# Second attention of a macaron block: value products issued inside the bursts, norm steps on GpSimd, no clearings, a squared term on VectorE

## What is computed

```python
q_norm_sq = jnp.sum(q * q, axis=-1, keepdims=True)
k_norm_sq = jnp.sum(k * k, axis=-1)[:, :, None, :]
qk = jnp.einsum('bhnd,bhmd->bhnm', q, k)
diff_sq = jnp.maximum(q_norm_sq + k_norm_sq - 2.0 * qk, 0.0)
denom = jnp.maximum((1.0 - q_norm_sq) * (1.0 - k_norm_sq), 1e-06)
cosh_arg = jnp.maximum(1.0 + 2.0 * diff_sq / denom, 1.0)
distance = arccosh(cosh_arg)
attn = jax.nn.softmax(-distance, axis=-1)
out = jnp.einsum('bhnm,bhmd->bhnd', attn, v)
```

## Time and profile before

| what | value |
|---|---|
| median of 3 runs | 3533.08 us (3528.67 to 3537.28) |
| the profiled execution's own time | 3532.39 us |
| its span | 3530.7 us |
| busy over the span: TensorE, VectorE, ScalarE, GpSimd | 2876.4, 2279.0, 1908.5, 850.3 us |
| mean granted clock of TensorE, as a share of full speed | 0.837 |
| the second attention (A1) in the span | about 1800 to 3090 us |
| its largest group, the GpSimd addition L1373, x96 in the page | 433.5 us, 4541 ns each |

### The profile page before, as it was taken

The page is one execution under the profiler, slowest core; times in us unless marked ns, Lnnn a source line. Parts: engine busy times, 40 slices in busy tenths (PEclk is TensorE's granted clock), DMA queues, the critical chain, the costliest instruction groups (busy, mean ns, idle before and its releaser), DMA issues. The chain is left out here.

```text
span 3530.7 us, 52885 instructions
## 1 busy us (share of the span) xinstructions
PE 2876.4 (81%) x17862; PEld 2183.2 (62%) x17862; DVE 2279.0 (65%) x5078; ACT 1908.5 (54%) x2244; POOL 850.3 (24%) x546
## 2 busy tenths in 40 slices
PE   5999968888599996999966767767676776679999
PEld 4888856666488885999952333333333333269998
DVE  5555557777555556666656776776676777366665
ACT  2222257676422222334318888887888888633333
POOL 1000010000000001000025555554655555410000
PEclk9999979999799997999975666666666666689999
DMA  2000000000000001000000000000000000010000
GB/s 78 0 0 0 0 1 1 0 0 0 0 1 0 0 0 48 0 0 0 0 0 0 1 1 0 0 0 0 0 0 0 0 0 0 0 48 0 0 0 24
DMA packets 3189, 17.98 MB, mean 5 GB/s; under 512 B 1088, under 2 KB 2112, under 8 KB 2112
## 3 DMA queue, kind: packets, MB, share of 16 engines
q1 hardware_dynamic: 3136, 17.32, 1.3%
HBM read 15.22 MB, written 2.10 MB: 5 GB/s over the span
## 5 line engine op out<-in xcount | busy, mean ns | idle before, releaser
L1373 POOL TENSOR_TENSOR A_Y<-A_Y,A_U 128x2048 f32<-128x2048 f32 x96 | 433.5, 4541 | 419.5 <-ACT A_U L1419 419.5
L1604 PE MATMUL ps<-A_QT,A_KT 9*128 9x512 f32 x512 | 294.3, 671 | 247.4 <-DVE A_U L1463 247.4
L1455 DVE TENSOR_SCALAR A_U<-ps 128x1024 f32<-128x1024 f32 x256 | 309.0, 1217 | 81.2 <-POOL A_Y L1373 50.4
L140 POOL TENSOR_TENSOR rstd<-var_eps,half_neg 128x4 f32<-128x4 f32 x45 | 49.8, 1107 | 1277.9 <-DVE var_eps L120 1277.9
L1604 PEld LDWEIGHTS ps<-A_QT,A_KT 9*128 9x128 f32 x512 | 120.0, 290 | 376.8 <-DVE A_U L1463 354.7
L1463 DVE SCALAR_TENSOR_TENSOR A_U<-ps,A_U 128x1024 f32<-128x1024 f32 x256 | 311.7, 1218 | 49.3 <-PE ps L1604 49.3
L1592 PE MATMUL ps<-A_QT,A_KT 28*128 28x512 f32 x512 | 269.7, 662 | 88.2 <-DVE A_U L1455 86.8
L257 ACT ACTIVATE F1b_act<-ps 128x512 f32<-128x512 f32 x256 | 153.3, 599 | 247.4 <-PE ps L223 231.4
L257 ACT ACTIVATE F1a_act<-ps 128x512 f32<-128x512 f32 x256 | 153.3, 599 | 242.9 <-PE ps L223 226.6
L257 ACT ACTIVATE F0b_act<-ps 128x512 f32<-128x512 f32 x160 | 95.7, 598 | 273.1 <-PE ps L223 273.1
L1419 ACT ACTIVATE A_U<-A_U 128x2048 f32<-128x2048 f32 x128 | 242.5, 1894 | 0.0
(11 more groups left out here) (334 smaller groups left out, 6673.0 us busy)
## 6 DMA issues: line engine op xcount, KB each, us to landing
dn<-in_down SPq DMA_DIRECT2D x2, 2048.0 KB, 12.0
stage<-in_up SPq DMA_DIRECT2D x1, 2560.0 KB, 9.2
X<-in_x SPq DMA_DIRECT2D x1, 2048.0 KB, 7.8
F1a_up<-in_up SPq DMA_DIRECT2D x1, 2048.0 KB, 7.8
F1b_up<-in_up SPq DMA_DIRECT2D x1, 2048.0 KB, 7.3
out_x<-X SPq DMA_DIRECT2D x1, 2048.0 KB, 6.3
dn<-in_down SPq DMA_DIRECT2D x1, 1280.0 KB, 11.9
qkv_w_s<-in_w_qkv SPq DMA_DIRECT2D x2, 192.0 KB
```

Source lines behind the costliest of these rows:

```text
L1373: eng.tensor_tensor(flat(y_slot(h)), flat(y_slot(h)), flat(Um[:, h % UR]), ALU.add).then_inc(s["t_ready"], 1)
L1455: eng.tensor_scalar(u_half(h, half), d_pair(n), 0.0, None, ALU.max).then_inc(s["dp_vector"], 1)
L1604: last = eng.matmul(ps[:, 4 + b, :], KT[r:r + 9, h // 2, kt * P:(kt + 1) * P], QT[r:r + 9, h // 2, :], start=True, stop=True)
```

## The change

In the second attention alone:

1. The value products of pairs 0, 2, 4 and 6 move from the stretch between the bursts into the burst before it (pair 0 into burst 1, 2 into burst 2, 4 into burst 3, 6 into the next pass's burst 0): a run of 8 behind half 5, another behind half 6. Pairs 1, 3, 5 and 7 stay between the bursts.
2. The residual sum goes to the buffer xa; GpSimd applies the norm (4 operations of 128 x 128) and copies the sum back to X. VectorE no longer applies the norm.
3. The clearings of the two tables go; TensorE, not VectorE, waits for `pad_ready`, before the first transposes.
4. Heads 4, 8 and 12 use the squared form.

```diff
-            SQUARED = ()
+            SQUARED = (4, 8, 12)
...
                 def square_on_vector(h):
-                    return h % 4 in SQUARED
+                    return h in SQUARED
...
+                def add_back_vector(eng, n, chunk):
+                    eng.wait_ge(s["o_done"], n)
+                    eng.tensor_tensor(xa[:, :].rearrange("p (t d) -> p t d", d=D), tiles_of(chunk),
+                                      ps[:, ROWS, :].rearrange("p (t d) -> p t d", d=D), ALU.add).then_inc(s["x_added"], 1)
+                    eng.drain()
+                    for t in range(TPC):
+                        eng.bn_stats(bn[:, t, :], xa[:, t * D:(t + 1) * D])
...
+                    eng.tensor_scalar(var_eps[:, :], mv[:, :, 1], EPS, None, ALU.add).then_inc(s["var_ready"], 1)
+
+                def apply_norm_gpsimd(eng, n, chunk):
+                    norm_gpsimd(eng, s, n)
+                    eng.drain()
+                    for t in range(TPC):
+                        eng.tensor_scalar(xn[:, t, :], xa[:, t * D:(t + 1) * D], mv[:, t, 0:1], rstd[:, t:t + 1],
+                                          ALU.subtract, ALU.mult)
+                    eng.drain().then_inc(s["xn_ready"], 1)
+                    eng.tensor_copy(tiles_of(chunk), xa[:, :].rearrange("p (t d) -> p t d", d=D))
+                    eng.drain()
...
                         eng.tensor_copy(xa[:, :], XT[:, 0:S]).then_inc(s["xa_ready"], 1)
-                        eng.memset(QA.rearrange("p h r -> p (h r)").bitcast(F32), 0.0)
-                        eng.memset(KA.rearrange("p h r -> p (h r)").bitcast(F32), 0.0)
-                        eng.memset(VA[:, :], 0.0)
-                        eng.drain()
                         eng.memset(QA[:, :, 26:28].bitcast(F32), 1.0)
...
+                        eng.memset(VA[:, :], 0.0)
+                        eng.drain()
...
                             if not first:
-                                norm_gpsimd(eng, s, c)
+                                apply_norm_gpsimd(eng, c, last_chunk(c))
...
                             if tail:
-                                residual_vector(eng, c, before_c)
-                                norm_stats_vector(eng, s, c, before_c)
+                                add_back_vector(eng, c, before_c)
                             out_copy_vector(eng, c, 0)
                             def after2(i):
-                                if tail and i == 1:
-                                    norm_apply_vector(eng, s, c, before_c)
...
-                        eng.wait_ge(pad_ready, 1)
                         take_q_vector(eng, 0, 6)
...
                             turn(c, EARLY)
-                            if not first:
-                                outputs(c - 1, 4, (0, 1))
                             turn(c, EARLY + 1)
-                            if not first:
-                                outputs(c - 1, 4, (2, 3))
...
                             def after0(i):
                                 if i < 4:
                                     turn(c, EARLY + 4 + i)
+                                if not first and i in (5, 6):
+                                    outputs(c - 1, 6, (2 * i - 10, 2 * i - 9))
...
                             if not first:
-                                outputs(c - 1, 6, (0, 1))
+                                outputs(c - 1, 7, (0, 1))
...
                             if not first:
-                                outputs(c - 1, 6, (2, 3))
-                                outputs(c - 1, 7, (0, 1, 2, 3))
+                                outputs(c - 1, 7, (2, 3))
...
                             def after1(i):
+                                if i in (5, 6):
+                                    outputs(c, 0, (2 * i - 10, 2 * i - 9))
...
-                            outputs(c, 0, (0, 1, 2, 3))
                             outputs(c, 1, (0, 1, 2, 3))
                             def after2(i):
+                                if i in (5, 6):
+                                    outputs(c, 2, (2 * i - 10, 2 * i - 9))
...
                             turn(c + 1, 0)
-                            outputs(c, 2, (0, 1))
                             turn(c + 1, 1)
-                            outputs(c, 2, (2, 3))
                             turn(c + 1, 2)
...
                             def after3(i):
                                 if i < 4:
                                     turn(c + 1, 4 + i)
+                                if i in (5, 6):
+                                    outputs(c, 4, (2 * i - 10, 2 * i - 9))
...
                         project_rows_tensor(eng, xa, 1, 7, "k_done")
+                        eng.wait_ge(pad_ready, 1)
```

More of the change, by code:

```diff
@@ L1169, in square_on_vector @@
                 def square_on_vector(h):
-                    return h % 4 in SQUARED
+                    return h in SQUARED
                 def squares(c, h):
-                    return c * (H // 4) * len(SQUARED) + len([i for i in range(h) if square_on_vector(i)])
+                    return c * len(SQUARED) + len([i for i in range(h) if square_on_vector(i)])
                 def flat(a):
@@ L1318, in early_bank @@
                     return (i + 2) % 6
-                (turn_out_tensor, divide_vector, turn_back_tensor, _, project_out_tensor,
-                 residual_vector) = tail_steps(s, lay, lambda t, g: OT[:, g, t * P:(t + 1) * P], on, oT, rden[:, :], ROWS)
+                (turn_out_tensor, divide_vector, turn_back_tensor, _, project_out_tensor, _) = tail_steps(s, lay, lambda t, g: OT[:, g, t * P:(t + 1) * P], on, oT, rden[:, :], ROWS)
                 def copy_back_vector(eng, n):
@@ L1332, in turn_norm_tensor @@
                     last.then_inc(s["tr_done"], 1)
+                def add_back_vector(eng, n, chunk):
[7 more added lines that the diff above has]
+                    for t in range(TPC):
+                        eng.bn_aggr(mv[:, t, :], bn[:, t, :])
+                    eng.drain()
[3 more added lines that the diff above has]
+                    eng.drain()
+                    for t in range(TPC):
+                        eng.tensor_scalar(xn[:, t, :], xa[:, t * D:(t + 1) * D], mv[:, t, 0:1], rstd[:, t:t + 1],
+                                          ALU.subtract, ALU.mult)
+                    eng.drain().then_inc(s["xn_ready"], 1)
+                    eng.tensor_copy(tiles_of(chunk), xa[:, :].rearrange("p (t d) -> p t d", d=D))
+                    eng.drain()
                 def copy_norm_vector(eng, n):
@@ L1398, in _ @@
                             main(c, False)
-                        norm_gpsimd(eng, s, B)
+                        apply_norm_gpsimd(eng, B, B - 1)
                         keep_norm_gpsimd(eng, B, B - 1)
@@ L1548, in _ @@
                         copy_back_vector(eng, B)
-                        residual_vector(eng, B, B - 1)
-                        norm_stats_vector(eng, s, B, B - 1)
-                        norm_apply_vector(eng, s, B, B - 1)
+                        add_back_vector(eng, B, B - 1)
                         copy_norm_vector(eng, B)
@@ L1720, in _ @@
                             main(c, False)
-                        for pair in range(4, PAIRS):
+                        for pair in range(5, PAIRS):
                             outputs(B - 1, pair, (0, 1, 2, 3))
```

## The result

| | before | after |
|---|---|---|
| median | 3531.01 us (4 runs) | 3577.85 us (3574.63 to 3582.62, 4 runs) |
| span of the profiled execution | 3530.7 us | 3572.9 us |
| busy: TensorE, VectorE, ScalarE, GpSimd | 2876.4, 2279.0, 1908.5, 850.3 | 2947.1, 2296.5, 1868.3, 903.3 |
| value products, 768 instructions | 176.2 us | 259.2 us |

The ratio is 1.0128 (interval 1.0114 to 1.0141): 1.3% slower, a small effect but clear of the noise. 3488 us was predicted, and even the range ended at 3548.

What follows compares the result with a forecast made beforehand. The prediction took the chain of VectorE with TensorE as the bound, ScalarE having slack. From 3532.4 us, -6.6 at the start, 7 passes at -5.7 and +1.7 at the end gave 3487.6, stated as 3488; range 3456 to 3548.

Steps and rivals of the forecast that it cites:

- rival B: Head 4's squared operation misses the border and VectorE sits through head 7's addition: +4.5 a pass, 3523.6 us; chance 0.18.
- rival D: Squared operation isn't held by GpSimd's additions, or first runs find the higher clock: 3466 us; chance 0.11.
- the rule that the prediction weighed: Elementwise work takes GpSimd about twice VectorE's time, so moving the norm would lose: total 3538 us.
- piece 3: From the statistics to burst 2: 5.8 us before, +3.0 forecast for the norm on GpSimd.
- rival E: Norm operations on GpSimd take 1.05 us each: +2.0 a pass, 3502 us; counted within the main forecast, no separate chance.
- The clock rises a run after dense work begins: In bursts, a moved pair's first run costs +2.0 less 0.3, its second +0.2; +1.5 per burst after a win-back.
- What is left at the higher clock: Stretches behind bursts 2 and 3: 7.8 us in place of 12.9 and 12.5, so -5.1 and -4.7.
- pieces 4, 6 and 8: Burst 2, burst 3, and burst 0 to the next origin: +0.5, +3.8 and -8.6 us forecast.
- rival C: Moved products no longer make a dense run, so TensorE's clock stays low: +10.4 a pass, 3605 us; chance 0.16.

Runs made afterwards that it cites:

- b_norm: Kernel before with only the norm applied by GpSimd: 3517.01 us, ratio 0.9954.
- b_noclear: Kernel before with only the clearings removed and TensorE rather than VectorE waiting for `pad_ready`: 3526.46 us, ratio 0.9987.
- b_moved: Kernel before with only the value products of pairs 0, 2, 4 and 6 moved into the bursts: 3513.51 us, ratio 0.9955.
- The first dose: a_keep with GpSimd's copy back done once more ahead of head 4's addition: 3508.04 us, ratio 0.9932.
- best1: Changed kernel without squared form, both runs of each moved pair side by side behind half 6, head 4's addition before GpSimd's norm: 3475.21 us.
- a_nosq: Changed kernel with no head in the squared form: 3521.99 us, ratio 0.9968.
- a_keep: Changed kernel with neither squared form nor moved products, leaving the norm on GpSimd and no clearings: 3509.68 us, ratio 0.9927.

## Why the prediction was wrong

**What bounds the kernel**: right. The chain is VectorE with TensorE; ScalarE had 40 us less to do (1868.3 against 1908.5 busy), and the kernel was slower all the same.

**The squared form**: sized right, for its own pieces. Head 4: request at 16.3, end at 19.5 forecast; 16.8 and 19.5 measured. Head 8: end at 11.1 into burst 2; 2539.49 + 4.12 - 2532.60 = 11.0. Head 12: +2.3; 2.29. So rival B (the border missed) and rival D (not held) are both out: VectorE waits for the addition under way and then runs its 2.3. GpSimd's next addition waits in its turn: four took 20.13 in place of 18.04 (head 7's ended at 23.9, 24.0 forecast) and two 11.08 in place of 9.01, which the prediction left out for head 8. The Trainium skill (SBUF — State Buffer, SBUF: two separate sides) has the port held for a whole instruction; these rows agree, in both directions.

**The norm on GpSimd**: the mechanism was right (b_norm gained 16 us against the rule that the prediction weighed, by which it would lose), but its term was too small. The forecast 3.1 was for the four operations, the copy back and the drains together; the four alone took 3.14 (795 ns each in the groups by line, not 547), and with copy and drains it was 4.3. With the inverse root's 1.05 and 0.3 of gaps around it, 5.6 us went by from the statistics to the addition and not 4.1, and piece 3 came 1.4 longer. That is most of rival E's +2.0, though not at its price of 1.05 each. The whole gain alone, 3.4 a pass, is close to the forecast 7.25 - 3.0.

**The clearings**: right. VectorE's wait before its first take fell from 12.11 to 5.72 us, -6.4 (forecast -6.6), and b_noclear gained 6.0.

**The step that failed** is the price of the moved products, in two terms. "The clock rises a run after dense work begins", from which the second run of a burst was taken at +0.2 (with 1.9 us for itself): it took 3.63 in bursts 2, 3 and 0, and 1.91 only in burst 1. And "What is left at the higher clock", in sum 7.8: 10.5 and 10.6 were measured, since the first run of the pair that stayed was slow again (2.96 and 3.63) and so were three and two of the transposes (1.11 in place of 0.66). Together with the slow second runs (+1.0, +2.3 and +2.5 in pieces 4, 6 and 8) this is 11 of the 12 us a pass. A warning stood in the rows of before: the earlier trace rows show one run of 3.38 ahead of ones of 1.91, but at a place where work stands side by side, and the change took just that away. The second term failed in b_moved too. The first one did not fail there, except in burst 1; what decides between the two kernels is not shown beyond the moments at which the runs start.

This is rival C, which had 0.16, though its condition (runs split by a factor don't raise the clock) held in three bursts of four here and in one of four in b_moved. Its 7.6 for second runs (5.8 came) and 4 for the stretches (5.5 came) are 11.6; without rival B's 4.5, which it included and which didn't come, it gives -5.7 + 11.6 = +5.9 a pass, and 3532.4 - 6.6 + 7 x 5.9 + 1.7 = 3568.8. Measured were +6.8 (passes of 160.1 and 160.75 in turn) and 3577.85. That the sum comes so near is in part luck, as its two terms miss in opposite directions. The page after has the value products at 83 us more of TensorE.

One thing no piece could show: the forecast moved all edges by what was added or removed. The first dose and best1 show that this kernel's edges don't follow one for one. That the squared form costs 56 to 78 us and that the moved products did not bring their forecast gain is shown by runs; that a_nosq comes out at 153.6 and a_keep at 150.2 rather than the reverse was read afterwards, and the rows of before would not have told it.

## What to carry to other kernels

Where TensorE works in patches and its clock is at 0.5 between them, the price of a run depends on what stands in front of it: before a run is moved, ask for both places whether the one that stays loses the work that kept the clock up. Give such a term the full range, here 1.9 to 3.6 us a run, and don't take one kernel's value for another's: the same split pair had a fast second run in three bursts of four in b_moved and in one of four in the changed kernel. Where parts of a change touch the same chain, measure them together too; their gains alone did not add up here. An engine with slack should not be relieved at the cost of the one on the chain: three roots less on ScalarE were worth nothing and three operations on VectorE cost 56 to 78 us.

## What was not expected of the hardware

The rise of TensorE's clock doesn't move one for one with the work: a run that started 0.79 us later ended only 0.37 later, and a cost of 0.75 us a pass on the chain vanished (pass 150.2 with and without it); of 4.4 us by which a run came earlier, 3.4 were lost again before the next pair was through. The pass often has one of a few lengths, 3.4 us apart, and one and the same edit is worth something else in each kernel: the products side by side gave -6.8 us a pass in one (39 us) and +3.4 in another (7 to 13 us).

Four operations of 128 x 128 took VectorE 7.25 us beside GpSimd's additions and 5.39 behind a squared operation, and GpSimd 3.14; free, VectorE does four of them in 1.11 (the same line in the profile after, ahead of the phase):

```profile
1794.17 1.11 DVE L126 TENSOR_SCALAR xn<-X,mv,rstd 128x128 f32<-128x128 f32 x4 [1.12 <-POOL rstd L140]
```
